# A linear attention layer with a ternary feed-forward: the order of the last batch's stages, the place of a norm in the queue, and the issuer of the stores

## What is computed

```
q = feature_map(split(x @ Wq.T + bq), orf)      # exp(proj - norm) + 1e-6, 128 features a head
k = feature_map(split(x @ Wk.T + bk), orf)
v = split(x @ Wv.T + bv)
kv = einsum('nlm,nld->nmd', k, v);  ksum = sum(k, axis=1)
out = einsum('nlm,nmd->nld', q, [kv, ksum])     # the last column is the divisor
out = out[..., :-1] / out[..., -1:]
x = layernorm(x + out @ Wo.T + bo)
w = clip(round(W / scale), -1, 1), scale = mean(|W|)
x = layernorm(x + x @ (w * scale).T)
```

## Time and profile before

| | |
|---|---|
| Median of 3 runs | 1280.61 us (1279.34 to 1284.43) |
| The profiled execution | 1279.7 us, of which the span of the instructions is 1277.9 |
| PE busy | 1258.1 us, 98% of the span |
| DVE / ACT / POOL busy | 900.1 / 712.0 / 358.6 us |
| Share of PE in the chain that ended last | 91% |
| Granted TensorE clock, mean | 0.999 of 2.4 GHz |

### The profile page before, as it was taken

One profiled execution on the slowest core, in us unless ns is written; L12 is line 12 of the kernel. 1 busy time (PEld: TensorE's weight loads), 2 busy tenths in 40 slices (PEclk: granted clock), 3 DMA queues, 4 the chain that ended last, 5 costly groups with the idle time before them and its releaser, 6 DMA issues.

```text
span 1277.9 us, 24908 instructions
## 1 busy us (share of the span) xinstructions
PE 1258.1 (98%) x8626; PEld 958.2 (75%) x8626; DVE 900.1 (70%) x1615; ACT 712.0 (56%) x1435; POOL 358.6 (28%) x745
## 2 busy tenths in 40 slices
PE   9999999999999999999999999999999999999986
PEld 8767787777877678776787768876788767886665
DVE  6589665786668865687657777577765787656766
ACT  5557536574356743667337763367544675356634
POOL 0112332124311333213422134311352123421143
PEclk9999999999999999999999999999999999999999
DMA  7658314772246821567215762258602775036611
GB/s 238 151 135 227 91 44 118 185 191 77 58 123 166 204 62 51 138 177 176 63 58 136 192 162 65 62 144 205 164 30 74 170 195 142 34 97 149 162 35 66
DMA packets 82748, 160.32 MB, mean 125 GB/s; under 512 B 17856, under 2 KB 36416, under 8 KB 82112
## 3 DMA queue, kind: packets, MB, share of 16 engines
q1 hardware_dynamic: 68880, 139.78, 43.6%
q10 hardware_dynamic: 9648, 16.85, 3.5%
q0 software_dynamic: 4096, 2.11, 0.7%
HBM read 39.13 MB, written 16.78 MB: 44 GB/s over the span
## 4 chain that ended last, share of the span: by engine, by line
PE 91%; DVE 2%; ACT 1%; issue 1%; POOL 0%; ACTq 0%; POOLq 0%; DVEq 0%
PE ps L953 27%; PE ps L916 21%; PE ps L1016 9%; PE ps L966 9%; PE ps L971 5%; PE ps L984 5%; PE ps L939 4%; PE ps L941 4%; PE ps L940 4%; PE ps L1042 2%; PE ps L993 1%; DVE stats L774 0%; PE ps L1001 0%; PE ps L1002 0%; ACT values_then_attention L624 0%
## 5 line engine op out<-in xcount | busy, mean ns | idle before, releaser
L676 ACT ACTIVATE features<-ps 128x512 f32<-128x512 f32 x512 | 277.8, 601 | 134.3 <-PE ps L966 129.4
L966 PEld LDWEIGHTS ps<-orf_stack,stacks 98*128 98x128 f32 x1024 | 130.8, 191 | 28.1 <-issue 20.3
L916 PE MATMUL ps<-Wo_hi,stacks 128*128 128x512 f32 x448 | 150.4, 402 | 0.0
L657 ACT ACTIVATE unit_hi<-ps,cols 128x512 fp32r<-128x512 f32 x128 | 88.4, 691 | 104.3 <-PE ps L953 104.3
L649 ACT ACTIVATE values_then_attention<-ps 128x512 f32<-128x512 f32 x64 | 38.2, 597 | 194.2 <-PE ps L941 192.1
L826 DVE SCALAR_TENSOR_TENSOR unit_lo<-ps,cols,unit_hi 128x512 fp32r<-128x512 f32 x128 | 94.0, 734 | 73.2 <-ACT squares L659 73.2
L790 DVE TENSOR_TENSOR den<-den,features 128x512 f32<-128x512 f32 x186 | 127.9, 688 | 10.8 <-ACT features L676 0.5
L568 POOL CAST norm_rows<-norms_turned 128x32 fp32r<-128x32 f32 x64 | 13.5, 212 | 432.9 <-DVE norms_turned L844 432.9
L552 POOL TENSOR_SCALAR stats<-stats 128x1 f32<-128x1 f32 x128 | 36.0, 281 | 338.3 <-DVE stats L777 338.1
L966 PE MATMUL ps<-orf_stack,stacks 98*128 98x128 f32 x1024 | 130.4, 272 | 0.0
L1016 PE MATMUL ps<-features,kv_ksum 128*32 128x512 f32 x1024 | 123.1, 598 | 2.6 <-ACT kv_ksum L697 1.6
(11 more groups left out here) (132 smaller groups left out, 2596.6 us busy)
## 6 DMA issues: line engine op xcount, KB each, us to landing
stacks<-unit_hi SPq DMA_DIRECT2D x512, 128.0 KB, 2.4
stacks<-unit_lo SPq DMA_DIRECT2D x256, 128.0 KB, 2.7
out<-rows ACTq DMA_DIRECT2D x56, 256.0 KB, 2.0
rows<-in_x_t SPq DMA_DIRECT2D x49, 256.0 KB, 3.4
rows<-in_x SPq DMA_DIRECT2D x32, 256.0 KB, 3.9
features<-in_x SPq DMA_DIRECT2D x32, 256.0 KB, 3.6
values_then_attention<-in_x_t SPq DMA_DIRECT2D x8, 256.0 KB, 6.7
stacks<-norm_rows POOLq DMA_DIRECT2D x128, 16.0 KB, 2.7
```

What stands on the lines that cost most here:

```text
L657: nc.scalar.activation(EH[:, u % 2, half], ps[:, :], ACT.Identity, bias=BC[:, u:u + 1]).then_inc(a_p.sem, 1)
L676: nc.scalar.activation(FE[:, n % 8, :, 0:M], ps[:, :].rearrange("p (a m) -> p a m", a=HG), ACT.Exp, scale=C_EXP).then_inc(a_exp.sem, 1)
L916: last = mm(out, a, b, start=(n == 0), stop=(n == len(terms) - 1))
L966: last = mm(ps[:, M * h:M * (h + 1)], slot[0:QK, L * h + P * r:L * h + P * (r + 1)], ORF[0:QK, h, :], start=True, stop=True)
```

## The change

Only stages of the last batch (b = 7) move; no product, copy or transfer is added or left out but for the last row, which is cut in two halves.

- Unit 5: KVT(2) comes ahead of F 4 and 5; S and L of the second half of unit 7 come behind F 6 and 7; F 0 and 1 of unit 6 come between GG(2,0) and GG(2,1); and Q(7,1), N(7), LIFT and NL come behind GG(2,1).
- Unit 7: GG(3,1), with DVE's part of it, comes ahead of OK(0,3), LN 0, OK(1,3), LN 1, where it stood behind A 3.
- Tail: Y(t-1) comes ahead of ST(t-4). Stores are issued by SP, which waits for `a_out`. The last row is normed in two halves, columns 0 to 255 by ACT, 256 to 511 by DVE, which waits only for POOL's second step, and is stored by two DMAs.

```diff
-            seq = f(0, 1) + p[0] + s0 + l0 + f(2, 3) + p[1] + q0 + f(4, 5) + half + p[2] + early + s1 + l1 + f(6, 7) + q1 + norm + lift + p[3]
+            seq = ([] if b + 1 == B and u + 2 == NU else f(0, 1)) + p[0] + s0 + l0 + f(2, 3) + p[1] + q0 + f(4, 5) + half + p[2] + early + s1 + l1 + f(6, 7) + q1 + norm + lift + p[3]
...
-        seq = p[0] + (s0 + l0 if b + 1 < B or u < NU - 3 else []) + splits + f(0, 1)
+        seq = p[0] + s0 + l0 + splits + f(0, 1)
...
-            seq += p[1] + s0 + l0 + kv + f(2, 3) + p[2] + f(4, 5) + s1 + q0 + [("KVT", b, g)] + f(6, 7) + l1 + [("GG", b, g, 0)] + q1 + norm + lift
-            seq += [("GG", b, g, 1), ("R", b, g, 0)] + [("LR", b, t) for t in range(4)]
+            seq += kv + f(2, 3) + p[1] + [("KVT", b, g)] + q0 + f(4, 5) + p[2] + f(6, 7) + s1 + l1 + [("GG", b, g, 0)]
+            seq += [("F", b, u + 1, 0), ("F", b, u + 1, 1), ("GG", b, g, 1)] + q1 + norm + lift
+            seq += [("R", b, g, 0)] + [("LR", b, t) for t in range(4)]
...
-        seq += [("R", b, g, 0, 1), ("AG", b, g, 0, 1), ("OK", b, 0, 3), ("LN", b, 0), ("OK", b, 1, 3), ("LN", b, 1), ("A", b, 2), ("A", b, 3)]
-        seq += [("GG", b, g, 1)] + [("OK", b, 2, k) for k in range(KT)] + [("LN", b, 2), ("Y", b, 0), ("A", b, 4)]
+        seq += [("R", b, g, 0, 1), ("AG", b, g, 0, 1), ("GG", b, g, 1), ("OK", b, 0, 3), ("LN", b, 0), ("OK", b, 1, 3), ("LN", b, 1)]
+        seq += [("A", b, 2), ("A", b, 3)] + [("OK", b, 2, k) for k in range(KT)] + [("LN", b, 2), ("Y", b, 0), ("A", b, 4)]
...
-        seq += o(t, 3) + [("LN", b, t)] + (o(t + 1, 0, 1, 2) if t + 1 < TT else []) + [("YT", b, t - 2), ("ST", b, t - 4), ("Y", b, t - 1), ("FF", b, t - 3)]
-    seq += [("YT", b, TT - 2), ("ST", b, TT - 4), ("Y", b, TT - 1), ("FF", b, TT - 3), ("YT", b, TT - 1), ("FF", b, TT - 2)]
+        seq += o(t, 3) + [("LN", b, t)] + (o(t + 1, 0, 1, 2) if t + 1 < TT else []) + [("YT", b, t - 2), ("Y", b, t - 1), ("ST", b, t - 4), ("FF", b, t - 3)]
+    seq += [("YT", b, TT - 2), ("Y", b, TT - 1), ("ST", b, TT - 4), ("FF", b, TT - 3), ("YT", b, TT - 1), ("FF", b, TT - 2)]
...
+                elif kind == "ST" and b + 1 == B:
+                    t = at[0]
+                    wait(a_out.sem, a_out.nth(b, t + 1))
+                    if is_last(b, t):
+                        sp.dma_start(out_tiles[b, t][:, 0:D // 2], last_rows[0]).then_inc(d_st[t % 4].sem, 16)
+                        wait(v_end, 1)
+                        sp.dma_start(out_tiles[b, t][:, D // 2:D], last_rows[1]).then_inc(d_end, 16)
+                    else:
+                        sp.dma_start(out_tiles[b, t], normed(b, t)).then_inc(d_st[t % 4].sem, 16)
...
+                    if is_last(b, u):
+                        act.wait_ge(g_ln[1].sem, g_ln[1].nth(b, 3 * u + 3))
+                        nc.scalar.activation(last_rows[0], last_rows[0], ACT.Identity, scale=ln(1, u, 10), bias=ln(1, u, 11))\
+                            .then_inc(a_out.sem, 1)
+                    else:
+                        apply_norm(1, b, u)
+                    if b + 1 < B:
+                        act.wait_ge(a_out.sem, a_out.nth(b, u + 1))
+                        act.dma_start(out_tiles[b, u], normed(b, u)).then_inc(d_st[u % 4].sem, 16)
...
+                    if is_last(b, u):
+                        dve.wait_ge(g_ln[1].sem, g_ln[1].nth(b, 3 * u + 2))
+                        nc.vector.tensor_scalar(last_rows[1], last_rows[1], ln(1, u, 6), ln(1, u, 10), ALU.subtract, ALU.mult)\
+                            .then_inc(v_end, 1)
```

More of the change, by code:

```diff
@@ L370, in attention_kernel @@
             "setup_bias_product", "setup_bias", "setup_w_abs", "setup_w_sum", "setup_w_scale", "setup_ternary"))
+        v_end, d_end = sem("last_half_ready"), sem("last_row_stored")
         s_pin, s_bld, s_ones = sem("carries_a_wait"), sem("setup_bo_loaded"), sem("setup_ones_written")
@@ L391, in normed, with is_last @@
             return XR[:, t % 4, :] if b + 1 < B else VA[:, t, :]
+        def is_last(b, t):
+            return (b, t) == (B - 1, TT - 1)
+        last_rows = [VA[:, TT - 1, D // 2 * h:D // 2 * (h + 1)] for h in range(2)]
         last_hi, last_lo = (X[:, :, :].rearrange("p k (s d) -> p (k s) d", d=D) for X in (XH, XL))
@@ L713, in _ @@
                 elif kind == "ST":
-                    apply_norm(1, b, u)
-                    act.wait_ge(a_out.sem, a_out.nth(b, u + 1))
-                    act.dma_start(out_tiles[b, u], normed(b, u)).then_inc(d_st[u % 4].sem, 16)
+                    if is_last(b, u):
[7 more added lines that the diff above has]
+                        act.dma_start(out_tiles[b, u], normed(b, u)).then_inc(d_st[u % 4].sem, 16)
             for sig in d_st:
                 act.wait_ge(sig.sem, sig.nth(B, 0))
+            act.wait_ge(d_end, 16)
         @block.vector
```

## The result

The changed kernel takes 1282.46 us as the median of 22 runs (1281.09 to 1286.11), the kernel before 1280.57 beside it. The ratio is 1.0014, with a 95% interval of 1.0008 to 1.0020: 1.8 us slower, where +0.4 had been predicted and rival 4 (the norm rows land late) had +1.9. That is within half a per cent and inside the range.

The account below looks back on a forecast made before the run. TensorE was taken as the bound, busy 98% of the span, with gains only in its last idle stretches. Terms +0.6 + 1.9 - 2.3 + 0.2 = +0.4 on 1280.6 gave 1281.0 us, range 1278.2 to 1283.5.

Parts of the forecast that it names:

- rival 4: Ahead of F 0 of unit 7, norm rows land in 4.5 us, not 2.9: sum +1.9, 1282.5 us; chance 0.10.
- Part A: Unit 5's order: 2.0 us gained at GG(2,0), lost by G(3,0), 0.5 late; norm rows 0.1 late; +0.6 us.
- Rival 3: TensorE's new 2.7 us idle ahead of G(3,0) brings the 1.2 GHz clock: +7 us, 1288; chance 0.03.
- Part B: Unit 7: GG(3,1) ahead of OK(0,3) waits for F 7's exponential on ACT and delays LN 2: +1.9 us.
- Rival 1: Delays of Part A and Part B aren't passed on (0 and +0.3): sum -1.8, 1278.8 us; chance 0.20.
- rival 2: Waits at GG(2,0), GG(2,1) and the 1.50 hole close: -6.6, 1274.0 us; chance 0.04, half of it 0.08.
- Part C: Tail: Y ahead of ST and stores on SP let YT(6) start sooner, then DVE's chain sets the end: -2.3 us.
- Part D: Last row in halves: ACT's half saves 0.3 us, SP's second DMA issue starts 0.55 later: +0.2 us.

Follow-up runs that it names:

- after_qn_first: The changed kernel with Q(7,1), N, LIFT and NL back ahead of two F tiles and GG(2,1); 1280.08 us, ratio 1.0001 to the kernel before.
- a_only: The kernel before with only unit 5's new order; 1282.31 us, ratio 1.0017 to the kernel before.
- after_fed: The changed kernel with 9 added matmuls on weights, result unused, filling TensorE's hole ahead of G(3,0); 1281.61 us, ratio 1.0009 to the kernel before.
- rows_late: The changed kernel with SP's four loads of x rows held back until F 0 of unit 7; 1281.76 us, ratio 1.0005 to the kernel before.
- fed_rows_late: The changed kernel with both 9 added matmuls ahead of G(3,0) and the four row loads held back; 1281.61 us, ratio 1.0005 to the kernel before.
- b_bias_first: The kernel before with GG(3,1) ahead of OK(0,3) and POOL's bias add of tile 2 ahead of the two scales; 1281.28 us, ratio 0.9998.
- b_only: The kernel before with only GG(3,1) moved ahead of OK(0,3); 1283.11 us, ratio 1.0022 to the kernel before.
- c_only: The kernel before with only Y ahead of ST in the tail, stores on ACT, last row whole; 1278.5 us, ratio 0.9984.
- cd_only: The changed kernel with unit 5's order and GG(3,1)'s move undone, leaving only the tail's changes; 1277.87 us, ratio 0.9983 to the kernel before.
- qn_first_no_b: As after_qn_first, with GG(3,1) also back behind A 3; 1278.75 us, ratio 0.9987 to the kernel before.
- bias_first: As qn_first_no_b, with POOL's bias add of tile 2 ahead of the scales of LN 0 and LN 1; 1276.68 us, ratio 0.9972 to the kernel before.

## Why the prediction was right, and where it wasn't

**Part A, the order:** right to 0.1 up to GG(2,1), and to 0.2 for G(3,0): +0.34 instead of +0.5, the hole 2.48 instead of 2.7. All of the gain at GG(2,0) was given back where the prediction put it, by Q and N behind GG(2,1) on DVE, and after_qn_first shows this as the cause (1.56 sooner).

**Part A, the size:** wrong. The term was the landing of the second norm DMA, taken at 2.9, between ends of 2.1 and 4.5. Its issue came where the plan had it (1210.5 in before's time). It took 4.5 in after and a_only and 4.3 in after_fed, which makes F 0 of unit 7 some 2.2 late; 0.35 of it is made up by GG(3,0), which the prediction didn't have. Part A is +1.85 up to GG(3,0) in a_only (0.35 + 1.85 - 0.35), and +2.0 timed, instead of +0.6. That is rival 4, which had 0.10 and 1282.5. The time lies inside the stated range because the range had this upper end in it; the central sum didn't foresee it. The median of all landings (2.7) was the wrong row to go by: it is a row of DMAs issued at other places. Why this one takes 4.5 isn't settled. Without the row loads beside it, it took 3.5 (rows_late, fed_rows_late). What the traces do show is where it stands: it was issued 0.9 behind the first row load's issue in after, a_only and after_fed (landing 4.3 to 4.5), 0.6 behind it in b_bias_first (3.8), and 0.1 ahead of it in before, b_only, c_only and cd_only (2.4 to 2.8). No run moved that issue alone, and what makes the landing 3.5 without any row load is open.

**Rival 3, the clock:** given 0.03, and the low clock is in the profile of after, though not at rival 3's price of 7 us. Not the whole of it counts, since up to F 0 of unit 7 the slow matmuls lay in a wait. What remained was 1.11 - (-0.44) = 1.6 in that execution. The reasoning that no idle up to 2.06 had brought the level down read too much into one execution (in which, besides, the 0.83 of 1274 to 1276 is followed by 0.50 to the end): in b_bias_first it fell behind one of 1.62, in qn_first_no_b behind one of 1.26. Of 90 timed runs of before, 38 are above 1280.7 us, nearly all of them at a mean clock of 0.996 to 0.998, and 52 at or below it, nearly all at 0.999, some 2 us apart. The 22 of after are all at 0.997 or less, a mean at which every profiled execution here has a low stretch ahead of PE's last matmul. So before seems to pay the clock in some executions and after in every one of them; its fastest run, 1281.09, is 1.75 above the fastest of before beside it.

**Part B:** right in place and size: idle of 2.10 (planned 2.4) ahead of GG(3,1), LN 0 2.36 late (2.0), LN 2 2.02 late (1.9), all of it passed to YT(2). b_only has +2.8 timed, of which 0.8 can be the clock. Rival 1 (soaked up) and rival 2 (the holes close) are out.

**Part C:** right, -2.24 for -2.3; YT(6) came right behind FF(4), and the rest is DVE's chain as laid out. The order alone gives 1.73 of it, the stores on SP the other 0.5. **Part D:** +0.14 for +0.2. Two terms of it were off and cancelled: SP's second issue came 0.44 behind the first, not 0.55, and took 0.37, so less than was read from loads; and POOL's last step took 0.39 instead of 0.26, beside DVE's half of the row. The Trainium skill (Trainium Kernel Development and Optimization, Key Constraints), by which moving a store saves only the issuer's time, has the trace on its side in the tail: the 0.5 is won on ACT's queue. For the last row, which was cut in two as well, no run parts the issuer from the halves.

**Sum:** 1.85 + 2.0 - 2.24 + 0.14 = +1.75, against +1.9 between the medians (+1.8 by the ratio). The prediction's +0.4 was 1.3 low by the one term of the landing. The rest, 0.1, is within the interval. The clock's share in the timed difference isn't settled: both kernels pay for it, before in fewer executions, and the profile of after_fed, at full clock, sums to +1.44, which would leave it some 0.4.

## What to carry to other kernels

When work moves earlier, list what is queued behind it on every other engine: here DVE took the sums of the second product ahead of two small steps that its own hole had hidden, and 2.0 us gained on TensorE became a loss. A DMA that ends a chain should be priced by the worst landing of its kind too and not by the median alone, above all when the change makes it the last to arrive. Swapping two steps in one engine's queue so that the one which feeds TensorE goes first was the only part that paid, 2 us for no work at all, and the same rule applied to GpSimd's bias add gave another 1.9.

## What the runs showed of the hardware

- TensorE's granted clock fell to the 1.2 GHz level at or behind idles of 1.26 (qn_first_no_b) and 1.36 (bias_first), both with one of 0.92 some 4 us ahead, 1.62 (b_bias_first), 2.06 (b_only), 2.10 (fed_rows_late), 2.34 (after_qn_first), 2.36 (b_only) and 2.48 us (after, a_only, rows_late), between 0.2 ahead of the idle's end (a_only) and 1.8 behind it (b_only). It stayed at 1.00 behind 1.61 and 2.06 in before, 2.10 and 2.35 in after and 2.37 in after_fed. The same idle does and doesn't bring it about from one execution to the next; only that of 2.48 did in all three kernels that have it, one execution each. The rule on idle gaps in the Trainium skill (TensorE: Matmul & The Clock Gate, Why this matters for your kernels) warns of longer ones; these rows show it for shorter ones.
- Of the DMAs of norm rows (16 KB) and the lifts (128 KB) that end in the same buffer, one landed 3.5 to 4.5 us after its issue in every kernel with the new unit 5: the norm rows where they were issued after the lifts (4.5, 4.3, and 3.5 without row loads), the last lift where they were issued before its end (4.1, 4.2, 3.8), while the other kind took 2.1 to 2.8. In before both took under 2.9; in b_bias_first, with the same order as before in that stretch, the norm rows took 3.8, so the order in the list alone doesn't decide it; there they were issued behind the first row load's issue and not ahead of it. No run moved that issue alone.
- GpSimd's last step took 0.39 us in all nine kernels in which VectorE works on the same row beside it, and 0.26 in the five others, before among them.
